# Cross term, table rows, squares and copies rearranged around a serial loop

## Chip, cores and metric

One core of a Trainium2 chip runs the whole program. The metric is the device time of one execution in microseconds (us). The kernel before takes 282.21 us (median of three runs, 282.20 to 282.55).

## What is computed

The input x is (1, 2048, 128). The reference chains four layers; the change touches the first and, by its place in the queues, the second.

```python
def step(M, kv):                     # 2048 tokens, one after the other
    k_t, v_t = kv
    v_pred = jnp.einsum('bf,bfd->bd', k_t, M)
    surprise = jnp.linalg.norm(v_t - v_pred, axis=-1, keepdims=True)
    delta = k_t[:, :, None] * v_t[:, None, :]
    M = M + eta_c[None, :, None] * surprise[:, :, None] * delta
    return (_ln2(M), None)           # subtract the mean, divide by the deviation
...
mem_out = jnp.einsum('btf,bfd->btd', q, M)      # q = phi(x_norm Wq)
output = x + jnp.einsum('btd,ed->bte', mem_out, Wout)
# then: expert layer (expert 1 of 16), h = relu(x W1 + b1), y = h W2 + b2
# then: causal attention with fractional rotary turns, one head
# then: a gated network with ternary weights, 128 -> 512 -> 512 -> 512 -> 128
```

## The kernel before

Tokens are the chunks of 128 of the large tiles x and xn (16 chunks); banks are the eight accumulation banks of TensorE, 512 fp32 each. The recurrence over 2048 tokens is replaced by 128 lanes (one on each partition) that each run over 32 tokens (L = 32), overlapping by 16, from products of keys and values. So the body is a loop of 32 steps in which every lane advances by one token, and what a step needs of the products is held in tables by lane.

Every engine has its own program, written out in order; semaphores join them. `o.did` counts an instruction on its engine's own semaphore and `need` waits for one. Around the change:

- **Before the steps.** TensorE brings the Gram products into lanes (L526) and ScalarE copies them into CC (L955). TensorE then multiplies the queries (L533, banks 4 and 5), turns xn (L540, banks 0 to 3), and computes the last rows (L544 to L549, bank 7). It runs eight warm-up matmuls (L445), which compute nothing that is read, and the eight expert-hidden matmuls (L561). ScalarE takes relu, relu of the negative and exp of the queries over both banks (L959 to L962), the first surprise (L970), the four copies of the turned xn into xT (L973), the last rows (L975 to L978), small rows of the tables (L987 to L991), and three of the eight hidden units (L984). VectorE forms lane rows of 32 elements (L1402 to L1410), four outer products (L1393, lines L1411 to L1415), the tables (L1419 to L1433), the near products (L1438), three far products that stay on VectorE (L1450) and row G (L1453).
- **A step j.** VectorE: near pairs (L1481), the scan over 18 rows of ST (L1504), the row of squares (L1486), alpha (L1518), the wide update of four rows (L1536), one diagonal element (L1491), for j < 13 the far product FP into a ring of three buffers (L1544), and the last pair (L1547). From step 13 on the near pairs follow the scan. ScalarE: square root (L1023), copy (L1025), the next surprise (L1028), which the next step's near pairs (from step 13 on its scan) wait for; then in steps 0 to 4 one hidden unit, and in some steps a piece of `behind`.
- **TensorE in the steps.** For j < 13 it adds FP of step j into bank 4 with an identity matmul (L608); VectorE may not rewrite a buffer of the ring before its matmul is done. Between them stand six pieces of `behind` (L577 to L587), which carry tables by one lane, and parts of the first expert output (L595 to L603). Behind them come L617, the three other expert outputs, and four warm-up matmuls for each of the steps 26 to 30. Step 13 of VectorE reads the sums of bank 4 (L1525, L1527).
- **After the steps.** TensorE's L636 waits for the last surprise; VectorE's L1554 waits for L636, and then a short exchange between the engines leads to the memory output (L623) and the attention.

The tiles: Cr holds four rows of 32 for each step, ST the 18 rows of the scan (R_G, R_T and so on are its row numbers), Y the pair sums, VC, aT, bT, V, KAP, FUS and Dv are tables and rows by lane; O1 to O4 and TA to TC are temporary squares of 16 x 32.

## Time and profile before

| | before |
|---|---|
| median of three runs | 282.21 us |
| the profiled execution | 282.72 us, span 280.9 us |
| TensorE matmuls busy | 264.1 us, 94% |
| VectorE busy | 219.0 us, 78% |
| ScalarE busy | 193.0 us, 69% |
| GpSimd busy | 98.5 us, 35% |
| mean granted clock of TensorE | 0.987 |
| chain that ended last | PE 67%, DVE 23%, ACT 4%, issue 3%, DMA 2% |

In the rows PE is TensorE's matmuls, PEld its weight loads, DVE VectorE, ACT ScalarE, POOL GpSimd. A busy share is a mean over stages that have different limits, so the stages have to be read one by one. In a timeline a row merges like instructions in sequence: their start, the time from the first start to the last end, and their count. An instruction's duration contains a latency that overlaps the next one's, so a cost in a queue is read from start to start. An fp32 matmul has two records. In a table of stretches the numbers after the length are busy time and count of PE, PEld, DVE, ACT and POOL, then TensorE's granted clock as a share of full speed.

### The profile page before, as it was taken

How to read it: one execution, taken by the hardware profiler on the slowest of the kernel's cores; microseconds unless marked ns; L12 is line 12 of the kernel's file. 1: busy time of each engine (PE TensorE's matmuls, PEld its weight loads, DVE VectorE, ACT ScalarE, POOL GpSimd, SP SyncE). 2: the span in 40 equal slices, each digit the busy share in tenths (PEclk: the TensorE clock that was granted, in tenths of full speed). 3: DMA queues.
4: the chain of work that ended last, by engine and by line, in shares of the span. 5: the costliest groups of instructions: out<-in, count | busy, mean ns of one | idle time of the engine just before them, and what ended most of it. 6: DMA issues, size and time to landing. Idle time of an engine off the chain costs nothing.

```text
span 280.9 us, 5415 instructions
## 1 busy us (share of the span) xinstructions
PE 264.1 (94%) x1799; PEld 170.1 (61%) x1803; DVE 219.0 (78%) x742; ACT 193.0 (69%) x469; POOL 98.5 (35%) x122
## 2 busy tenths in 40 slices
PE   6899898899999889979999999999999999999993
PEld 2369863354645544746877777787695444444482
DVE  6977389999998689589999988778852766666684
ACT  1587469865456459778865799999674877777730
POOL 9210000000000055998885469898872000000000
PEclk9999979999999979999999999999999999999999
DMA  8700000000000091300000000000000000000005
GB/s 204 199 13 2 2 2 1 0 1 0 2 1 1 13 387 54 128 23 1 2 2 0 0 2 1 3 0 0 0 2 2 0 0 1 2 1 0 0 10 144
DMA packets 8287, 8.51 MB, mean 30 GB/s; under 512 B 1729, under 2 KB 7362, under 8 KB 7746
## 3 DMA queue, kind: packets, MB, share of 16 engines
q1 hardware_dynamic: 7826, 7.84, 8.7%
q10 hardware_dynamic: 432, 0.30, 0.4%
q8 instruction: 16, 0.26, 0.4%
q14 instruction: 13, 0.11, 0.1%
HBM read 7.09 MB, written 1.05 MB: 29 GB/s over the span
## 4 chain that ended last, share of the span: by engine, by line
PE 67%; DVE 23%; ACT 4%; issue 3%; DMA 2%; SPq 0%; DVEq 0%; ACTq 0%
PE PS L826 10%; PE PS L827 10%; PE PS L784 10%; PE PS L764 9%; PE PS L775 4%; PE PS L480 3%; PE PS L499 3%; DVE arena L1536 2%; DVE arena L1481 2%; PE PS L741 2%; PE PS L742 2%; PE PS L704 2%; PE PS L445 2%; DMA x<-L_attn_x 2%; DVE arena L1518 1%
## 5 line engine op out<-in xcount | busy, mean ns | idle before, releaser
L826 PE MATMUL PS<-arena 128*128 128x512 f16 x128 | 48.5, 379 | 0.6 <-issue 0.6
L827 PE MATMUL PS<-arena 128*128 128x512 f16 x128 | 48.5, 379 | 0.0
L1768 DVE TENSOR_TENSOR arena<-arena 128x512 f32<-128x512 f32 x32 | 22.2, 692 | 19.5 <-ACT arena L1203 19.5
L764 PE MATMUL PS<-arena 128*128 128x512 f32 (+3 forms) x80 | 32.0, 531 | 0.0
L1202 ACT ACTIVATE arena<-PS,arena 128x512 f32<-128x512 f32 x32 | 22.0, 688 | 13.1 <-PE PS L827 13.1
L1251 POOL CAST arena<-arena 128x512 f16<-128x512 f32 x2 | 1.2, 612 | 78.9 <-ACT x L1064 78.9
L1243 POOL TENSOR_TENSOR arena<-arena 128x256 f32<-128x256 f32 x32 | 21.6, 674 | 15.5 <-DVE arena L1707 13.2
L1176 ACT ACTIVATE arena<-PS,lnt 128x512 f32<-128x512 f32 (+3 forms) x40 | 25.0, 635 | 1.8 <-DVE lnt L1722 1.7
L1244 POOL TENSOR_TENSOR arena<-arena,small 128x256 f16<-128x256 f32 (+1 forms) x36 | 23.8, 662 | 2.8
L1715 DVE TENSOR_REDUCE mxb<-PS 128x1 f32<-128x512 f32 (+3 forms) x40 | 22.1, 602 | 1.6 <-PE PS L766 1.6
L826 PEld LDWEIGHTS PS<-arena 128*128 128x128 f16 x128 | 12.5, 98 | 15.7 <-issue 0.7
L1203 ACT ACTIVATE arena<-PS,arena 128x512 f16<-128x512 f32 x32 | 21.8, 682 | 0.0
L827 PEld LDWEIGHTS PS<-arena 128*128 128x128 f16 x128 | 12.5, 98 | 15.0
L764 PEld LDWEIGHTS PS<-arena 128*128 128x128 f32 x80 | 14.0, 190 | 11.7 <-issue 9.5
L775 PE MATMUL PS<-con,arena 128*128 128x128 f32 x136 | 19.6, 274 | 0.5 <-ACT arena L1176 0.5
L784 PE MATMUL PS<-arena,xn 128*128 128x128 f32 x144 | 19.3, 279 | 0.4 <-ACT xn L1160 0.3
L784 PEld LDWEIGHTS PS<-arena,xn 128*128 128x128 f32 x144 | 17.4, 191 | 1.4 <-ACT xn L1160 1.1
L784 PE MATMUL PS<-arena 128*128 128x128 f32 x128 | 17.3, 279 | 0.3 <-ACT arena L1160 0.2
L775 PEld LDWEIGHTS PS<-con,arena 128*128 128x128 f32 x136 | 15.1, 141 | 3.7 <-issue 1.7
L1699 DVE SCALAR_TENSOR_TENSOR arena<-arena,PS 128x256 f32<-128x256 f32 x32 | 13.4, 420 | 4.6 <-ACT arena L1133 3.9
L445 PE MATMUL PS<-warm 128*128 128x512 bf16 x49 | 13.6, 413 | 3.5 <-POOL warm L1223 1.3
L1700 DVE SCALAR_TENSOR_TENSOR arena<-PS,arena 128x256 f32<-128x256 f32 x32 | 15.5, 484 | 1.1
(282 smaller groups left out, 638.0 us busy)
## 6 DMA issues: line engine op xcount, KB each, us to landing
arena<-h_T SPq DMA_DIRECT2D x2, 1024.0 KB, 5.5
x<-L_attn_x SPq DMA_DIRECT2D x4, 256.0 KB, 4.6
arena<-cos SPq DMA_DIRECT2D x1, 1024.0 KB, 4.8
arena<-sin SPq DMA_DIRECT2D x1, 1024.0 KB, 7.0
out<-arena SPq DMA_DIRECT2D x4, 256.0 KB, 2.3
arena<-w_T SPq DMA_DIRECT2D x3, 256.0 KB, 2.9
con<-shape_constants ACTq DMA_DIRECT2D x1, 192.0 KB, 3.4
w1e<-L_ffn_W SPq DMA_DIRECT2D x1, 128.0 KB
```

The source lines that it names most:

```text
L764: i = mm(PS[:, k, 0:cnt * P], qT1[:, t * P:(t + 1) * P], kT1[:, c * P:(c + cnt) * P], start=True, stop=not last)
L775: i = tr(PS[:, 4 + gi % 2, (b - c) * P:(b - c + 1) * P], Pr[t % 2][:, b * P:(b + 1) * P], ident)
L784: i = mm(PS[:, 7, (t % 4) * D:(t % 4 + 1) * D], PT[t % 2][:, b * P:(b + 1) * P], V1[:, b, :], start=(b == 0), stop=(b == t))
L826: mm(bank(u % 8), wH[:, k, m * P:(m + 1) * P], sH[:, k, cols], start=(k == 0), stop=False)
L827: i = mm(bank(u % 8), wL[:, k, m * P:(m + 1) * P], sL[:, k, cols], start=False, stop=(k == HT4 - 1))
L1176: f(Pr[t % 2][:, c * P:(c + cnt) * P], PS[:, SCORE_BANK[gi], 0:cnt * P], ACT.Exp, scale=1.0 / D, bias=nbs[:, t:t + 1], accum_out=rsums[:, ...
L1202: f(FP[u % 4], bank(u % 8), ACT.Gelu, scale=s_[:, u % HT4:u % HT4 + 1])
L1203: f(high, bank(u % 8), ACT.Gelu, scale=s_[:, u % HT4:u % HT4 + 1]).then_inc(read, 1)
L1243: o.need(o.did(tt(rest, value, high, ALU.subtract)))
L1244: return tt(low, rest, low_scale.broadcast_to([P, cols]), ALU.mult)
L1715: i = did(v.tensor_reduce(mxb[:, gi:gi + 1], PS[:, SCORE_BANK[gi], 0:cnt * P], AX.X, ALU.max))
L1768: v.tensor_tensor(RP[m], FP[m], high, ALU.subtract).then_inc(rest_ready, 1)
```

## The change

The cross term of the mean (a V D products, formerly TA, O2 and the row built from them for all pairs) is no longer formed as a table: Cr row 1 is built from aT and VC alone, a new row R_W of ST holds the other factor, a new row R_M receives the product in the last operation of each step, which becomes three columns wide, and the next surprise reads R_M instead of R_D. Row R_CD of ST is made by VectorE from two small operations. Rows 2 and 3 of Cr are sums of two squares each, now added by TensorE with identity matmuls into banks 2 and 3 and copied by ScalarE. The row of squares and the diagonal element become one operation over two rows of the arena, for which ST is moved next to Cr. On ScalarE the query relus are split by bank, the four copies into xT and all eight hidden units go into the steps 0 to 8, and the pieces of `behind` two steps later. On TensorE the second half of the hidden matmuls follows the far products of the steps 0 to 3; the last rows (bank 6 now) follow L617, and ScalarE copies them in the steps 15 to 18.

The diff, cut:

```diff
@@ -352,8 +354,13 @@
         LANE_RUNS = [(0, 5), (5, 5), (10, 5), (15, 2)]
 
 
-        BEHIND_AT = {4: (0,), 5: (1,), 6: (2,), 8: (3,), 9: (4,), 10: (5,)}
+        BEHIND_AT = {6: (0,), 7: (1,), 8: (2,), 10: (3,), 11: (4,), 12: (5,)}
+        EXPERT_AT = {0: (("x", 0), ("x", 1)), 1: (("x", 2), ("h", 0)), 2: (("x", 3), ("h", 1)), 3: (("h", 2),), 4: (("h", 3),), 5: (("h", 4),), 6: (("h", 5),), 7: (("h", 6),), 8: (("h", 7),)}
+        LAST_AT = 15
         BEHIND_BANK = (5, 6, 7, 5, 6, 7)
+
+
+        TERM_BANK = (2, 3)
 
         def values_in(engine, ch):
...
                     i = mm(PS[64 * hf:64 * hf + F, 4 + b, :], wqT[:, :], xrT[:, ch * BANK:(ch + 1) * BANK], start=True, stop=True)
-            i.then_inc(q_done, 1)
+                i.then_inc(q_done, 1)
+
+            def table(k):
+
+                b = TERM_BANK[k]
+                for i in range(2):
+                    if i == 0:
+                        pe.wait_ge(lanes_act, b + 1)
+                    pe.wait_ge(terms_ready, 2 * i + k + 1)
+                    p = mm(bank(b), ident, (O4, O3, TC, TB)[2 * i + k].rearrange("p j t -> p (j t)"), start=(i == 0), stop=(i == 1))
+                p.then_inc(terms_done, 1)
+
+            table(0)
+            table(1)
 
             pe.wait_ge(xn_ready, NT)
             for n in range(NT):
                 if n % 4 == 0:
                     pe.wait_ge(lanes_act, n // 4 + 1)
+                    if n // 4 in TERM_BANK:
+                        pe.wait_ge(terms_act, TERM_BANK.index(n // 4) + 1)
...
-
-            pe.wait_ge(mrow_ready, 1)
-            mm(PS[0:L, 7, F + 2 * D:F + 2 * D + 1], lane[:, MM, :], con[:, C_ID + LAST:C_ID + LAST + 1], start=True, stop=True).then_inc(last_done, 1)
-
             keep_warm(8, 6)
             pe.wait_ge(moe_in, 64)
-            for h in range(2):
-                for ch in range(4):
-                    if h == 0:
-                        pe.wait_ge(xnt_act, ch + 1)
-                    if (h, ch) == (0, 0):
-                        pe.wait_ge(qphi_act, 2)
-                    if (h, ch) == (0, 3):
-                        pe.wait_ge(last_act, 4)
-                    mm(bank((4, 0)[h] + ch), w1e[:, h * P:(h + 1) * P], xT[:, ch * BANK:(ch + 1) * BANK], start=True, stop=True).then_inc(eh_done, 1)
+
+            def expert_hidden(h, ch):
+
+                pe.wait_ge(xnt_act, ch + 1)
+                mm(bank((4, 0)[h] + ch), w1e[:, h * P:(h + 1) * P], xT[:, ch * BANK:(ch + 1) * BANK], start=True, stop=True).then_inc(eh_done, 1)
...
@@ -602,19 +618,28 @@
                         for h in range(2):
                             mm(PS[:, c, (n % 4) * P:(n % 4 + 1) * P], HT[:, h, n * P:(n + 1) * P], w2e[:, h, :], start=False, stop=False)
 
-            pe.wait_ge(eh_act, 4)
             for j in range(FAR):
+                pe.wait_ge(eh_act, min(j + 1, 4))
                 pe.wait_ge(fp_ready, j + 1)
                 mm(PS[:, FAR_BANK, j * HALF:(L - 1) * HALF], ident, FPf[j % N_FP][:, 0:(L - 1 - j) * HALF], start=(j == 0), stop=(j == FAR - 1)).then_inc(far_done, 1)
+                if j < 4:
+                    expert_hidden(1, j)
                 for k in BEHIND_AT.get(j, ()):
                     behind(k)
                 if j in EO_EARLY:
-                    pe.wait_ge(eh_act, 8)
+                    pe.wait_ge(eh_act, 5 if EO_EARLY[j][1] == 1 else 8)
                     expert_output(0, *EO_EARLY[j])
 
             pe.wait_ge(small_in, 16 * 13)
             pe.wait_ge(behind_act, 9)
             mm(PS[:, 7, 0:D], wvT2, wo, start=True, stop=True).then_inc(wvo_done, 1)
+            tr(PS[0:L, 6, 0:F], KU[F:P, SH - 2, 1, :], con[F:P, C_ID + F:C_ID + P])
+            mm(PS[0:L, 6, F:F + D], VT[:, T - L:T], woutT[:, :], start=True, stop=True)
+            mm(PS[0:L, 6, F + D:F + 2 * D], ones[:, 0:L], woutT[:, :], start=True, stop=True).then_inc(last_done, 1)
+
+            pe.wait_ge(mrow_ready, 1)
+            mm(PS[0:L, 6, F + 2 * D:F + 2 * D + 1], lane[:, MM, :], con[:, C_ID + LAST:C_ID + LAST + 1], start=True, stop=True).then_inc(last_done, 1)
+
             def memory_output(two, first, end):
...
 
-            zq = PS[:, 4:6, :].rearrange("p b c -> p (b c)")
+            def relus(b, negative):
+
...
+
+                act.wait_ge(terms_done, k + 1)
+                have = bank(TERM_BANK[k]).rearrange("p (j t) -> p j t", t=L)
+                if k == 0:
+                    f(Cr[:, 0:HALF, 2, 0:L - 1], have[:, :, 1:L], ACT.Copy).then_inc(terms_act, 1)
+                else:
+                    f(Cr[:, 0:HALF, 3, :], have, ACT.Copy).then_inc(terms_act, 1)
+
             act.wait_ge(q_done, 1)
-            f(QT, zq, ACT.Relu).then_inc(qphi_act, 1)
-            n = o.did(f(QE, zq, ACT.Relu, scale=-1.0))
+            n = relus(0, True)
+            relus(0, False)
             o.need(n)
-            f(QE, QE, ACT.Exp, scale=-1.0).then_inc(qphi_act, 1)
+            f(QE[:, 0:BANK], QE[:, 0:BANK], ACT.Exp, scale=-1.0).then_inc(qphi_act, 1)
+            act.wait_ge(q_done, 2)
+            n = relus(1, True)
+            o.need(n)
+            f(QE[:, BANK:2 * BANK], QE[:, BANK:2 * BANK], ACT.Exp, scale=-1.0).then_inc(qphi_act, 1)
+            table(0)
 
             def surprise(j):
...
             act.wait_ge(lanes_act, 1)
             f(surprise(0), CC[:, 2, 1, 0:1].broadcast_to([W, SCAN // STEP]), ACT.Sqrt).then_inc(g_ready, 1)
-            for ch in range(4):
+            table(1)
+            act.wait_ge(terms_act, 1)
+            o.did(f(lane[:, VB, 0:HALF], of_tables(2), ACT.Square))
+            o.did(f(ST[:, R_C, PAD:PAD + HALF], of_tables(2), ACT.Copy, scale=2.0))
+            act.wait_ge(terms_act, 2)
+            o.did(f(ST[:, R_B, PAD:PAD + HALF], of_tables(3), ACT.Copy, scale=0.5))
+            n = o.did(f(lane[:, T0, 0:HALF], of_tables(3), ACT.Relu, scale=0.5))
+            assert n == STATICS
+            relus(1, False)
+
+            def last_rows(i):
+
+                if i == 0:
+                    act.wait_ge(last_done, 2)
+                to, have, scale = ((U_LAST, PS[0:L, 6, 0:F], 1.0), (VW, PS[0:L, 6, F:F + D], 1.0), (WSUM, PS[0:L, 6, F + D:F + 2 * D], 1.0),
+                                   (negm, PS[0:L, 6, F + 2 * D:F + 2 * D + 1], -1.0))[i]
+                f(to, have, ACT.Copy, scale=scale).then_inc(last_act, 1)
+
+            def normed_turned(ch):
+
                 act.wait_ge(xnt_done, ch + 1)
                 f(xT[:, ch * BANK:(ch + 1) * BANK], bank(ch), ACT.Copy).then_inc(xnt_act, 1)
-            act.wait_ge(last_done, 2)
-            f(U_LAST, PS[0:L, 7, 0:F], ACT.Copy).then_inc(last_act, 1)
-            f(VW, PS[0:L, 7, F:F + D], ACT.Copy).then_inc(last_act, 1)
-            f(WSUM, PS[0:L, 7, F + D:F + 2 * D], ACT.Copy).then_inc(last_act, 1)
-            f(negm, PS[0:L, 7, F + 2 * D:F + 2 * D + 1], ACT.Copy, scale=-1.0).then_inc(last_act, 1)
-
...
-            act.wait_ge(tables_ready, 1)
-            o.did(f(lane[:, VB, 0:HALF], of_tables(2), ACT.Square))
-            o.did(f(ST[:, R_C, PAD:PAD + HALF], of_tables(2), ACT.Copy, scale=2.0))
-            o.did(f(ST[:, R_B, PAD:PAD + HALF], of_tables(3), ACT.Copy, scale=0.5))
-            o.did(f(ST[:, R_CD, PAD:PAD + HALF], of_tables(1), ACT.Copy))
-            n = o.did(f(lane[:, T0, 0:HALF], of_tables(3), ACT.Relu, scale=0.5))
-            assert n == STATICS
             act.wait_ge(moe_in, 64)
-            for u in range(8 - EH_LATE):
-                hidden(u // 4, u % 4)
 
             def behind(k):
...
                     act.wait_ge(h_ready, j + 1)
                     f(surprise(j + 1), HS[:, j + 1:j + 2].broadcast_to([W, SCAN // STEP]), ACT.Sqrt,
-                      scale=of_scan(R_D), bias=AL[:, j:j + 1]).then_inc(g_ready, 1)
-                if j < EH_LATE:
-                    hidden((8 - EH_LATE + j) // 4, (8 - EH_LATE + j) % 4)
+                      scale=of_scan(R_M), bias=AL[:, j:j + 1]).then_inc(g_ready, 1)
+                for what, i in EXPERT_AT.get(j, ()):
+                    (normed_turned(i) if what == "x" else hidden(i // 4, i % 4))
+                if 0 <= j - LAST_AT < 4:
+                    last_rows(j - LAST_AT)
                 if j == SB_AT:
...
-            did(v.tensor_tensor(R[FD], FUS, Dv, ALU.mult))
-            did(v.tensor_tensor(R[KD], KAP, Dv, ALU.mult))
             did(v.tensor_scalar(R[WJ], Dv, float(1.0 / np.sqrt(D)), None, ALU.mult))
-            last()
+            need(fd)
+            did(v.tensor_scalar(R[MZ], R[FD], float(-np.sqrt(D)) / N, None, ALU.mult))
+            mr = did(v.tensor_scalar(R[MR], R[FD], -2.0 / N / N, None, ALU.mult))
             v.tensor_scalar(R[MM], R[FD], 1.0 / N, None, ALU.mult).then_inc(mrow_ready, 1)
-            did(v.tensor_scalar(R[MZ], R[FD], float(np.sqrt(D)) / N, None, ALU.mult))
-            did(v.tensor_scalar(R[M2], R[FD], 2.0 / N, None, ALU.mult))
-            did(v.tensor_scalar(R[MR], R[FD], -2.0 / N / N, None, ALU.mult))
-            did(outer(O1, Dv, R[VB]))
-            need(o.n - 1)
-            did(outer(O2, R[M2], R[KD]))
-            did(outer(O3, R[MR], R[FD]))
-            did(outer(O4, R[MZ], KAP))
+            did(v.tensor_scalar(ST[:, R_W, PAD:PAD + L - 1], Dv[:, 1:L], float(-2.0 / np.sqrt(D)), None, ALU.mult))
+            need(mr)
+            outer(O4, R[MZ], KAP).then_inc(terms_ready, 1)
+            outer(O3, R[MR], R[FD]).then_inc(terms_ready, 1)
+            o1 = did(outer(O1, Dv, R[VB]))
             dve.wait_ge(lanes_act, 4)
-            outers = o.n
-            need(outers)
-            ab = did(v.tensor_tensor(TA, aT, V, ALU.mult))
+            v.tensor_tensor(TC, aT, R[WJ][:, 0:HALF].unsqueeze(2).broadcast_to(SQUARE), ALU.mult).then_inc(terms_ready, 1)
+            v.scalar_tensor_tensor(out=TB, in0=bT, scalar=2.0 / N, in1=V, op0=ALU.mult, op1=ALU.mult).then_inc(terms_ready, 1)
+            need(o1)
             vc = did(v.scalar_tensor_tensor(out=VC, in0=V, scalar=2.0, in1=O1, op0=ALU.mult, op1=ALU.subtract))
-            bv = did(v.tensor_tensor(TB, bT, V, ALU.mult))
-            aw = did(v.tensor_tensor(TC, aT, R[WJ][:, 0:HALF].unsqueeze(2).broadcast_to(SQUARE), ALU.mult))
             did(v.tensor_copy(VJ[:, 0:HALF], diagonal(2)))
+            square = did(v.tensor_tensor(R[T1][:, 0:HALF], diagonal(0, 1), diagonal(0, 1), ALU.mult))
             need(vc)
             half = did(v.tensor_scalar(vc_diagonal, vc_diagonal, 0.5, None, ALU.mult))
-            square = did(v.tensor_tensor(R[T1][:, 0:HALF], diagonal(0, 1), diagonal(0, 1), ALU.mult))
-            did(v.scalar_tensor_tensor(out=Cr[:, 0:HALF, 1, 0:L - 1], in0=TA[:, :, 1:L], scalar=-2.0, in1=O2[:, :, 1:L], op0=ALU.mult, op1=ALU.add))
-            need(bv)
-            c1_ = did(v.scalar_tensor_tensor(out=Cr[:, 0:HALF, 3, :], in0=TB, scalar=2.0 / N, in1=O3, op0=ALU.mult, op1=ALU.add))
-            need(aw)
-            v.tensor_tensor(Cr[:, 0:HALF, 2, 0:L - 1], TC[:, :, 1:L], O4[:, :, 1:L], ALU.subtract).then_inc(tables_ready, 1)
-            need(c1_)
+            need(half)
+            v.scalar_tensor_tensor(out=Cr[:, 0:HALF, 1, 0:L - 1], in0=aT[:, :, 1:L], scalar=-1.0, in1=VC[:, :, 1:L], op0=ALU.mult, op1=ALU.mult).then_inc(tables_ready, 1)
             statics = did(v.tensor_tensor(R[T1][:, 0:HALF], R[T1][:, 0:HALF], vc_diagonal, ALU.mult))
 
             for j in range(HALF - 2):
...
 
+            dve.wait_ge(tables_ready, 1)
+            dve.wait_ge(terms_act, 1)
+            cross = did(v.tensor_tensor(R[WT][:, 0:HALF], ST[:, R_W, PAD:PAD + HALF], of_tables(2), ALU.mult))
             for j in range(FAR, HALF):
                 did(v.tensor_tensor(OJF[j - FAR], *far_factors(j), ALU.mult))
+            need(cross)
+            did(v.tensor_tensor(ST[:, R_CD, PAD:PAD + HALF], R[WT][:, 0:HALF], of_tables(1), ALU.add))
             need(statics)
             dve.wait_ge(act_order, STATICS)
...
             def query_sums(*pieces):
 
-                dve.wait_ge(qphi_act, 2)
+                dve.wait_ge(qphi_act, 4)
                 for q in pieces:
...
-                def row_of_squares():
+                def squares():
 
                     need(added)
-                    return did(v.tensor_tensor(Cr[:, j, 0, j + 1:end - 1], CC[:, 0, j + 1, j + 2:end], Y[:, j, j + 2:end], ALU.mult))
-
-                def diagonal_term():
-
-                    need(added)
-                    did(v.tensor_tensor(ST[:, R_T, PAD + j + 1:PAD + j + 2], CC[:, 0, j + 2, j + 2:j + 3], Y[:, j + 1, j + 2:j + 3], ALU.mult))
+                    a0 = cr_at + j * 4 * L + j + 1
+                    apart = st_at + R_T * RW + PAD + j + 1 - a0
+                    both = arena[:, a0:a0 + 2 * apart].rearrange("p (l t) -> p l t", l=2)[:, :, 0:end - j - 2]
+                    return did(v.tensor_tensor(both, CC[:, 0, j + 1:j + 3, j + 2:end], Y[:, j:j + 2, j + 2:end], ALU.mult))
 
                 if j == HALF:
...
-                    diagonal_term()
                 if j < FAR:
 
...
                                            op0=ALU.mult, op1=ALU.mult).then_inc(fp_ready, 1)
                 need(formed)
-                formed = did(v.tensor_tensor(ST[:, R_X:R_SQ + 1:STEP, PAD + j + 1], ST[:, R_R, PAD + j + 1:PAD + j + 2].broadcast_to([W, 2]),
-                                             ST[:, R_C:R_R + 1, PAD + j + 1], ALU.mult))
+                formed = did(v.tensor_tensor(ST[:, R_X:R_M + 1:STEP, PAD + j + 1], ST[:, R_R, PAD + j + 1:PAD + j + 2].broadcast_to([W, 3]),
+                                             ST[:, R_C:R_W + 1, PAD + j + 1], ALU.mult))
                 if Q_AT <= j < Q_AT + 6:
```

## Rows read from the trace of the kernel before

**Rows 1.** Chain of work, 83 to 92 us: start us, us, engine, tile, line

```profile
86.56 4.25 PE PS L445 x19
...
90.81 0.21 PE PS L636 x2
```

**Rows 2.** Stretches: length, busy us (x instructions) by engine, PEclk, DMA share, GB/s

```profile
51.60:67.30 15.70, 14.45 (x45) 7.21 (x43) 15.70 (x88) 11.82 (x46) 0.00 (x0) 1.00 0.00 1
...
67.30:90.80 23.50, 23.40 (x110) 13.26 (x112) 21.98 (x137) 12.55 (x56) 0.00 (x0) 1.00 0.01 1
```

**Rows 3.** Timeline of ScalarE: table load, copies, second step, last root

```profile
42.65 1.28 ACT L970 ACT_TABLE_LOAD   x1
...
44.05 2.04 ACT L973 ACTIVATE xT<-PS 128x512 f32<-128x512 f32 x4
...
50.07 0.20 ACT L1023 ACTIVATE arena<-arena 128x1 f32<-128x1 f32 x1
...
50.66 0.67 ACT L984 ACTIVATE arena<-PS,b1e 128x512 f32<-128x512 f32 x1
...
89.96 0.40 ACT L1028 ACTIVATE arena<-arena 128x6 f32<-128x6 f32 x1
```

**Rows 4.** Timeline of TensorE: start us, us, engine, line, operation, operands, xcount, [idle before]

```profile
44.73 7.10 PE L561 MATMUL PS<-xT,w1e 128*128 128x512 f32 x16 [0.71 <-issue]
...
51.67 2.58 PE L608 MATMUL PS<-arena,con 128*128 128x496 f32 x6
...
67.96 1.02 PE L597 MATMUL PS<-xn,con 128*128 128x512 f32 x2
...
72.08 1.02 PE L595 MATMUL PS<-x,con 128*128 128x512 f32 x2
```

**Rows 5.** Timeline of VectorE before the steps

```profile
35.88 0.18 DVE L1402 TENSOR_SCALAR arena<-arena 128x32 f32<-128x32 f32 x1 [1.55 <-ACT arena L955]
...
36.73 2.49 DVE L1393 TENSOR_TENSOR arena<-arena 128x512 f32<-128x512 f32 x4
...
39.33 0.69 DVE L1419 TENSOR_TENSOR arena<-arena 128x512 f32<-128x512 f32 x1
...
43.87 2.21 DVE L1438 TENSOR_TENSOR arena<-arena 128x210 f32<-128x210 f32 x14
...
46.00 1.14 DVE L1450 TENSOR_TENSOR arena<-arena 128x288 f32<-128x288 f32 x3
...
47.62 0.44 DVE L1481 SCALAR_TENSOR_TENSOR arena<-arena 128x210 f32<-128x210 f32 x1 [0.21 <-DVE arena L1453]
```

**Rows 6.** Timeline of VectorE in the second step

```profile
49.52 0.41 DVE L1481 SCALAR_TENSOR_TENSOR arena<-arena 128x182 f32<-128x182 f32 x1
...
50.46 0.15 DVE L1491 TENSOR_TENSOR arena<-arena 128x1 f32<-128x1 f32 x1
...
50.53 0.71 DVE L1544 SCALAR_TENSOR_TENSOR arena<-arena 128x480 f32<-128x480 f32 x1
...
51.23 0.38 DVE L1481 SCALAR_TENSOR_TENSOR arena<-arena 128x156 f32<-128x156 f32 x1
```

**Rows 7.** Timeline of VectorE in a late step

```profile
83.75 0.25 DVE L1536 SCALAR_TENSOR_TENSOR arena<-arena 128x28 f32<-128x28 f32 x1
...
83.91 0.15 DVE L1491 TENSOR_TENSOR arena<-arena 128x1 f32<-128x1 f32 x1
...
84.03 0.16 DVE L1547 TENSOR_TENSOR arena<-arena 128x2 f32<-128x2 f32 x1
```

**Rows 8.** Timeline of TensorE, the block L544 to L549

```profile
41.37 0.23 PE L544 MATMUL PS<-con,arena 64*32 64x64 f32 x1
...
41.99 0.20 PE L549 MATMUL PS<-con,arena 128*32 128x1 f32 x2
```

**Rows 9.** Stretches around the fall of TensorE's granted clock

```profile
33.70:34.50 0.80, 0.08 (x2) 0.06 (x2) 0.62 (x2) 0.39 (x2) 0.00 (x0) 1.00 0.00 0
...
34.80:38.00 3.20, 3.20 (x19) 2.36 (x19) 2.09 (x11) 1.94 (x4) 0.00 (x0) 0.50 0.00 0
```

33 lines of the change are left out of this document (20 added, 13 removed).

## The prediction

> **What bounds the kernel now.** I read the chain of work in order of time first. From 35.9 to 86.56 us nearly every link is a VectorE instruction, and then, before the last step ends, the chain crosses to TensorE: 4.25 us of warm-up matmuls (L445), and only then L636, which releases the next VectorE instruction [rows 1]. So two engines have to be followed. The table of stretches says the same: VectorE is busy throughout 51.6 to 67.3, while TensorE has 1.3 us of idle there; from 67.3 to 90.8 TensorE is busy for 23.40 of 23.50 us [rows 2]. TensorE's queue is full from the last far product on, through the expert outputs and twenty warm-up matmuls (20 x 512 columns back to back, 4.27 us), and ends at 90.81, 0.4 us after ScalarE wrote the last step's root (89.96 + 0.40 [rows 3]), for which L636 waits as well. Both ends are nearly tied; a change that frees VectorE alone gains nothing behind 67.3 unless TensorE's queue too is shorter or starts earlier.
>
> TensorE's order is fixed: eight expert-hidden matmuls (L561) from 44.73 to 51.67, 0.85 us each; thirteen far products (L608) with the six pieces of `behind` and one expert matmul between them, to 67.96; then expert outputs from 67.96 on, the last three from 72.08 [rows 4].
>
> **VectorE before the steps.** Before: eight lane operations of 0.1 from 35.88, four outer products from 36.73 at 0.60 pitch, seven 512-wide ones, `near`, OJF, and the first step at 47.62 [rows 5]. The change has seven lane operations (fd, VB, WJ, MZ, MR, MM, R_W), three outers, and TC, TB, VC, Cr1: seven 512-wide operations in place of eleven. That is 4 x 0.60 = 2.4 less, 0.1 less of lane work and about 0.1 less of waiting for the outers; against it stand the new wait of Cr1 for `half` (0.1), and two 16-wide operations, cross and CD (0.2). New walk: O4 36.52, O3 37.12, O1 37.72, TC 38.32, TB 38.92, VC 39.52, small ones 40.13, Cr1 40.55, near 41.23, OJF 43.45, CD 44.5, G 44.6, and the first step at 45.0. It begins 2.6 us earlier.
>
> It needs ScalarE and TensorE to follow. The two table rows are now four identity matmuls of 0.85 in the queue behind the query matmuls: 39.47 to 42.9. ScalarE's work on the queries ended at 42.65 [rows 3]; now the first bank is released by itself, about 1.0 earlier, and the last relu (0.5) moves behind the rows, so it is free at about 41.2. It copies row 2 at 41.4 (TensorE's end of it) to 42.0, then pays the load of the square root's tables (1.28, as before [rows 3]) to 43.3, copies row 3 to 44.0, and ends the four small rows at 44.4, 0.2 before VectorE asks. So the cover is thin: were the tables 0.5 late, the first step would be 0.3 late. TensorE turns xn at 42.9 to 44.8 and warms up to 46.5.
>
> **The steps 0 to 12.** One step is 49.52 to 51.23 = 1.71 us, and the diagonal takes 0.07 of it (50.46 to the far product at 50.53) [rows 6]. Without it 1.65. The pair of squares reads up to 14 more elements, 0.01, beside the wait for alpha; the third column of the last operation I take at nothing (it has 2 elements now). For VectorE alone: 13 x 0.06 = 0.8.
>
> But now the four copies of xT are in ScalarE's part of the steps. In a step ScalarE starts at the scan's end (50.07) and is free for a copy 0.59 later (50.66) [rows 3]. The copy of x takes 0.5 (2.04 for four), a hidden one 0.57. Scan 0 ends at 45.55: x0 46.17 to 46.75, x1 to 47.25. Scan 1: x2 47.83 to 48.40, h0 to 48.97. Scan 2 ended at 48.82, so ScalarE comes at 48.9: x3 49.50 to 50.10.
>
> **TensorE behind that.** First hidden matmul at 46.85 where it was 44.73, that is 2.1 later. Three of them run to 49.41, then TensorE waits 0.7 for x3. From 50.17 its queue has no gap, by my walk: hidden(0,3) and the four of the second half, 5 x 0.853 = 4.27; the far products, 496 to 304 columns in steps of 16, 5200 columns at 1.67 ns (2.41 us for the first 1440, L608's row of six less its tail of 0.17) = 8.7; `behind` 2240 columns by the same rate, plus 0.4 for the floors of its three narrow ones = 4.2; the expert's first matmul 0.85. In sum 13.7, ending at 68.1. The other bound of that work is what the table shows for it: 14.45 busy [rows 2] and 0.61 for the last far product = 15.1, in which short pauses each leave a tail and a restart. I take 13.7, since the new queue has no such pauses.
> The ring of three far buffers now holds VectorE: L1544 of step 3 waits for the matmul of step 0, which ends at 51.9, where it would be ready at 51.0. ScalarE also waits in step 10 for the third piece of `behind`. Both delays cost nothing, because the far sums in step 13 wait for TensorE's 68.0 anyway (VectorE would be there at 66 to 67). Read at 68.2, where they were read at 68.46, they leave 0.3 of the vector gain of 3.4.
>
> **The steps 13 to 30.** There the diagonal costs nothing now: the last operation starts at 84.03, just when the wide one ends (83.75 + 0.25), and the diagonal at 83.91 lies inside [rows 7]. Taking it out gives 0. The squares, on the path here, grow by 16 elements falling to 1, 136 in all: at about 1 ns, +0.14. The vector chain ends 0.2 earlier than now.
>
> A rule of the Trainium skill ("Perfetto Trace Analysis", Optimizing Scalar/DVE Operations) says that grouping small vector operations raises throughput where the engine is saturated. By it all thirty merged diagonals would count, 2 us at 0.07. The trace agrees for the first thirteen [rows 6] and shows nothing to gain in the rest [rows 7].
>
> **The block that moves.** L544 to L549, 0.82 us (41.37 to 42.19) [rows 8], ran where TensorE had slack and now stands behind L617, in the full stretch. ScalarE's four small copies of it go into steps 15 to 18; it may wait for the block until 73.3 in step 15, 0.1 behind its normal start and within the slack before alpha. They cost nothing. The matmuls cost their whole 0.82.
>
> **The sum.** TensorE: 50.17 + 4.27 + 13.7 + 22.85 (67.96 to 90.81, unchanged work) + 0.82 = 91.8, where L636 now starts at 90.81. So +1.0 us. All that follows hangs on L636 and shifts as a whole. The profiled execution took 282.72 (span 280.9), so it would be 283.7; against the median of 282.21 that gives **283.2**. With a vector walk off by 0.3 either way, the matmuls 0.2 cheaper or 1.4 dearer: 282.8 to 284.6.
>
> **Rivals.**
> *Vector gains carry* (7%). If TensorE made up its late start, the end would follow VectorE: 2.6 + 0.8 + 0.2 for step 0, where ScalarE was late, less 0.1: 3.5 faster, 278.7. It decides at the far sums: TensorE must end L608 by 65, that is 50.2 to 65 for 18 us of matmuls. For it speaks that VectorE is the busier engine up to 67.3; against it the columns. A half form, in which x3 comes before 49 and pauses in the second half that I took for work vanish, gives 280 to 281.6. The same skill section has it that work may well go from a saturated VectorE to another engine; that is this rival, and it holds only if that other engine has room.
> *The tie absorbs it* (14%), 282.0 to 282.7. The late start is 0.5 less than I say and the 0.82 block falls partly into a gap in the new queue (TensorE waiting for VectorE near step 12).
> *ScalarE is late* (11%). It is a link in everything: two relus, table copies, table load and small rows, with 0.2 of cover; then two copies a step. If x3 comes 0.8 to 1.5 later: 284.0 to 284.8.
> *TensorE's clock* (8%). After its pause from 33.7 to 34.5 the granted clock is 0.50, the lower of its two levels (1.2 GHz), from 34.8 to 38.0 [rows 9]. The change puts pauses of 0.35 and 0.7 before a stretch that TensorE bounds. One such fall costs half of 3.3 us: +1.6, 284.8 to 285. Against it: the pause of 0.7 before 44.73 has no fall behind it. The Trainium skill ("TensorE: Matmul & The Clock Gate", Part 1) states that idleness throttles the array and activity releases it; the trace agrees [rows 9], and the rule speaks against moving the copies that feed the matmuls.
> *The tables are no faster summed by TensorE* is within the third.
>
> **How the numbers follow.** Forecast 60% (282.8 to 283.9 within it). The range from 282.2 to 284.7 leaves out the faster rival, the clock and a part of the third: under 2 in 10. A measurement can tell about 0.2%, 0.56 us: faster 0.07, same 0.15, slower 0.78.
>
> **What would show it.** The first step near 45.0 (L1481 before); L561's first at 46.9 and a pause of about 0.7 before its fourth; from 50.2 to L636 a TensorE without idle; L1544 of the fourth step with idle before it, released by TensorE; far sums read near 68.2; the moved block near 72.4, and L636 near 91.8. Wrong it would be if TensorE has idle between 52 and 68, if the first hidden matmul starts before 46, or if the warm-up matmuls in front of L636 start on a scan and not on the end of the expert outputs.

## Result and profile after

The changed kernel takes 283.89 us (median of 5 runs, 283.68 to 284.29), the kernel before 282.21 (5 runs, 282.03 to 282.55). The ratio is 1.0058, with a 95% interval of 1.0044 to 1.0073: it is slower, by 1.7 us. The profiled execution of after took 283.77, span 282.0.

The profile's page of after gives its busy times and its chain by engine:

```profile
PE 265.2 (94%) x1807; PEld 170.0 (60%) x1811; DVE 215.8 (77%) x709; ACT 193.2 (69%) x473; POOL 98.4 (35%) x122
...
PE 77%; DVE 13%; ACT 5%; issue 2%; DMA 2%; SPq 0%; DVEq 0%; ACTq 0%
```

The stretches of after (columns as in [rows 2]): first the pause and the stretch behind it that answer to [rows 9], then from the fourth hidden matmul to the reading of the far sums, and from there to the matmul that was L636 and is now L661:

```profile
33.70:34.50 0.80, 0.09 (x2) 0.02 (x1) 0.66 (x2) 0.39 (x2) 0.00 (x0) 1.00 0.00 0
34.80:38.00 3.20, 3.20 (x25) 1.71 (x23) 2.25 (x10) 2.56 (x6) 0.00 (x0) 1.00 0.00 0
...
50.20:68.30 18.10, 18.10 (x55) 9.91 (x56) 15.19 (x75) 13.50 (x49) 0.00 (x0) 1.00 0.00 0
68.30:92.20 23.90, 23.85 (x117) 13.66 (x116) 20.55 (x113) 12.94 (x59) 0.00 (x0) 1.00 0.00 1
```

TensorE is busy for 18.10 of 18.10 us and then for 23.85 of 23.90. VectorE, which was busy for all of 51.6 to 67.3 before [rows 2], is now busy for 15.19 of 18.10. The bound has gone wholly to TensorE.

The timeline of TensorE in after (columns as in [rows 4]):

```profile
37.90 3.86 PE L550 MATMUL PS<-arena,con 128*128 128x512 f32 x8
41.60 1.91 PE L562 MATMUL PS<-con,xn 128*128 128x128 f32 x16
43.56 1.67 PE L452 MATMUL PS<-warm 128*128 128x512 bf16 x7
47.10 2.81 PE L572 MATMUL PS<-xT,w1e 128*128 128x512 f32 x6 [1.86 <-ACT xT L1037]
50.19 1.13 PE L572 MATMUL PS<-xT,w1e 128*128 128x512 f32 x2 [0.27 <-ACT xT L1037]
51.15 1.00 PE L624 MATMUL PS<-arena,con 128*128 128x496 f32 x2
...
68.47 1.05 PE L613 MATMUL PS<-xn,con 128*128 128x512 f32 x2
...
72.71 0.23 PE L636 MATMUL PS<-con,arena 64*32 64x64 f32 x1
...
73.46 1.13 PE L611 MATMUL PS<-x,con 128*128 128x512 f32 x2
...
88.03 4.26 PE L452 MATMUL PS<-warm 128*128 128x512 bf16 x19
92.22 0.28 PE L661 MATMUL PS<-con,arena 128*32 128x1 f32 x2
```

The expert-hidden matmuls start at 47.10 where they started at 44.73 [rows 4], and TensorE stands 1.86 us for ScalarE's first copy of xT. The matmul that all else hangs on (L636 before, L661 after) is called the decisive one below. The chain of work has it at 90.81 in before [rows 1], but a timeline counts its start a little earlier. As all starts below are from timelines, the row to compare with is this one of before:

```profile
90.74 0.28 PE L636 MATMUL PS<-con,arena 128*32 128x1 f32 x2
```

So the decisive matmul starts at 92.22 instead of 90.74, 1.48 later. From there to the end of the span the kernels take nearly the same: 190.16 us before, 189.78 after.

VectorE in after: the outer products, the last wide table operation, the first step, the far product of the fourth step, the far sums, and the closing operation of a late step. They answer to [rows 5] and [rows 7]:

```profile
36.37 1.89 DVE L1444 TENSOR_TENSOR arena<-arena 128x512 f32<-128x512 f32 x3
...
41.07 2.21 DVE L1481 TENSOR_TENSOR arena<-arena 128x210 f32<-128x210 f32 x14
...
44.83 0.44 DVE L1529 SCALAR_TENSOR_TENSOR arena<-arena 128x210 f32<-128x210 f32 x1 [0.22 <-DVE arena L1501]
...
52.18 0.68 DVE L1587 SCALAR_TENSOR_TENSOR arena<-arena 128x448 f32<-128x448 f32 x1 [1.42 <-PE PS L624]
...
65.80 0.23 DVE L1529 SCALAR_TENSOR_TENSOR arena<-arena 128x6 f32<-128x6 f32 x1 [1.07 <-ACT arena L1077]
...
68.48 0.51 DVE L1571 SCALAR_TENSOR_TENSOR arena<-arena,PS 128x288 f32<-128x288 f32 x1 [0.19 <-PE PS L624]
...
83.26 0.17 DVE L1590 TENSOR_TENSOR arena<-arena 128x3 f32<-128x3 f32 x1
```

ScalarE in after, answering to [rows 3]: table load, the first step with two copies of xT behind its root, the last copy, the last step's root:

```profile
40.68 1.28 ACT L1015 ACT_TABLE_LOAD   x1
...
45.79 0.20 ACT L1072 ACTIVATE arena<-arena 128x1 f32<-128x1 f32 x1 [2.15 <-DVE arena L1550]
...
46.38 1.06 ACT L1037 ACTIVATE xT<-PS 128x512 f32<-128x512 f32 x2
...
49.56 0.57 ACT L1037 ACTIVATE xT<-PS 128x512 f32<-128x512 f32 x1
...
90.31 0.40 ACT L1077 ACTIVATE arena<-arena 128x6 f32<-128x6 f32 x1
```

VectorE enters the steps 2.8 us earlier (44.83 for 47.62) and loses all of it, and what the merging saves in the steps too: 1.42 at L1587 for a far buffer, some 0.1 before the same operation in each of the next five steps, 1.07 in the thirteenth step for ScalarE, and 0.19 before the far sums, which are read at 68.48. VectorE has to wait for TensorE there.

**One caution on the clock.** The granted clock of TensorE differs between executions of one and the same program. The profiled execution of before has two stretches of 3.4 us at half clock (called falls below), [rows 9] and one from 99.7 to 103; that of after has none. Over the 97 runs of the kernel before that stand beside the experiments, those with a mean clock of 0.998 or more took 281.4 to 282.4 us, those with 0.983 to 0.985 283.7 to 284.2. So below I read the start of the decisive matmul beside the median.

Runs of like clock can also be compared alone. At 0.998 or more, the 24 such runs of the kernel before have a median of 281.87, and the three of after took 283.68 to 283.89. That is 1.9 us, more than the 1.7 of the medians.

### The profile page after: what moved, and what is told of

Its sections match the earlier page's. It is cut to its first block, busy times and chain, and to the rows that moved or that the text cites. A ratio compares the mean times of both kernels' runs of the same rounds, so it can differ in the third digit from the quotient of the medians.

```text
span 282.0 us, 5418 instructions
## 1 busy us (share of the span) xinstructions
PE 265.2 (94%) x1807; PEld 170.0 (60%) x1811; DVE 215.8 (77%) x709; ACT 193.2 (69%) x473; POOL 98.4 (35%) x122
## 4 chain that ended last, share of the span: by engine, by line
PE 77%; DVE 13%; ACT 5%; issue 2%; DMA 2%; SPq 0%; DVEq 0%; ACTq 0%
PE PS L851 10%; PE PS L852 10%; PE PS L809 10%; PE PS L789 9%; PE PS L800 4%; PE PS L624 3%; PE PS L487 3%; PE PS L619 3%; PE PS L506 3%; PE PS L766 2%; PE PS L767 2%; PE PS L452 2%; PE PS L572 2%; DMA x<-L_attn_x 2%; PE PS L615 1%
## 5 line engine op out<-in xcount | busy, mean ns | idle before, releaser
L452 PE MATMUL PS<-warm 128*128 128x512 bf16 x49 | 14.2, 426 | 3.8 <-POOL warm L1274 1.3
```

## Experiments

The theory, called T in the expectations, is the forecast's: TensorE's queue decides, its late start costs some 2 us, the moved block its own 0.8, and what VectorE gains goes nowhere. The kernel before, run beside each of the three groups of experiments, had medians of 282.26, 282.33 and 282.32 us; after stands at 283.89.

**The block moved back** in front of the hidden matmuls, with its four copies in front of the steps:

```diff
+            tr(PS[0:L, 7, 0:F], KU[F:P, SH - 2, 1, :], con[F:P, C_ID + F:C_ID + P])
...
             keep_warm(8, 6)
...
             mm(PS[:, 7, 0:D], wvT2, wo, start=True, stop=True).then_inc(wvo_done, 1)
-            tr(PS[0:L, 6, 0:F], KU[F:P, SH - 2, 1, :], con[F:P, C_ID + F:C_ID + P])
...
             act.wait_ge(moe_in, 64)
+            for i in range(4):
+                last_rows(i)
```

> Against the changed kernel (283.89 us median). The last rows' four matmuls go back in front of the warm-ups before the steps (bank 7), and ScalarE copies them in its pause before step 0. Theory T (TensorE's queue sets the end from its fourth hidden matmul to L661): the block took 0.75 us of that queue (72.71 to 73.46), so L661 starts 0.75 earlier, at 91.5, and the time is 283.1. Rival V (VectorE's chain or ScalarE's late copies set the end, and the block lies in a gap): 0.0, 283.9.

Measured: 282.77 us (12 runs, 282.33 to 283.47), ratio to before 1.0014 [0.9999, 1.0030]. The timeline of TensorE:

```profile
46.70 2.81 PE L579 MATMUL PS<-xT,w1e 128*128 128x512 f32 x6 [0.63 <-ACT xT L1039]
...
91.07 0.28 PE L663 MATMUL PS<-con,arena 128*32 128x1 f32 x2
```

The decisive matmul is 1.15 earlier than in after (92.22), and the median 1.1 lower. The pause in front of the hidden matmuls has shrunk from 1.86 to 0.63: the block ran inside it. Of the 1.15, 0.19 came in by the fourth hidden matmul, which starts at 50.00 for 50.19, since ScalarE, busy with small rows just before, answered the first scan at once (in after it did not). The rest, 0.96, is the block. Its own matmuls took 0.75 in after (72.71 to 73.46), and some 0.2 more lay in the distances from L635 to the block (0.32, where L635 and the next matmul are 0.22 apart here) and from L611 to L613 behind it (0.96 for 0.86).

**The four copies of xT in front of the steps again**, one of the eight hidden units in each of the first eight steps:

```diff
-        EXPERT_AT = {0: (("x", 0), ("x", 1)), 1: (("x", 2), ("h", 0)), 2: (("x", 3), ("h", 1)), 3: (("h", 2),), 4: (("h", 3),), 5: (("h", 4),), 6: (("h", 5),), 7: (("h", 6),), 8: (("h", 7),)}
+        EXPERT_AT = {0: (("h", 0),), 1: (("h", 1),), 2: (("h", 2),), 3: (("h", 3),), 4: (("h", 4),), 5: (("h", 5),), 6: (("h", 6),), 7: (("h", 7),)}
...
             act.wait_ge(moe_in, 64)
+            for ch in range(4):
+                normed_turned(ch)
```

> Against the changed kernel (283.89). The four copies of the turned xn go back before step 0, into ScalarE's pause from 43.6 to 45.8; the hidden units follow one a step from step 0. Theory T: the first hidden matmul starts when the warm-ups end, 45.25 where it was 47.10, and the pause before the fourth disappears, so the fourth starts at 47.8 where it was 50.19; all behind it in TensorE's queue is 2.4 earlier, and the time is 281.5. If only the later start counts and the pause comes back elsewhere: 1.85 earlier, 282.0. Rival V (VectorE's steps set the end): its steps 0 to 12 begin no earlier, 283.6 to 283.9.

Measured: 281.20 us (12 runs, 280.9 to 284.7), ratio 0.9976 [0.9950, 1.0003]. TensorE, then VectorE behind the decisive matmul:

```profile
45.10 3.60 PE L572 MATMUL PS<-xT,w1e 128*128 128x512 f32 x8
...
89.61 0.28 PE L661 MATMUL PS<-con,arena 128*32 128x1 f32 x2
```

```profile
65.87 0.52 DVE L1573 SCALAR_TENSOR_TENSOR arena<-arena,PS 128x288 f32<-128x288 f32 x1 [0.19 <-PE PS L624]
...
89.93 0.15 DVE L1599 COPY arena<-PS 32x1 f32<-32x1 f32 x1 [1.54 <-PE PS L661]
```

The hidden matmuls start 2.00 earlier than in after, and the pause before the fourth is gone; the decisive one starts 2.61 earlier, and the median falls by 2.69. No warm-up and no operation of VectorE was taken out. So the copies' place alone is worth more than the whole loss of the change. The interval of the ratio still reaches just over 1; the runs at a clock of 0.998 or more took 281.12 to 281.23, against the 281.87 of before and the 283.77 of after (medians at that clock). VectorE still waits 1.54 for TensorE at the end: more gain of VectorE would give nothing here either.

**Both undone together.**

> Both edits, the block in front of the warm-ups and the copies before step 0. Theory T: 0.75 and 2.4 add up only if the block doesn't push the hidden matmuls; it does so by 0.75 (the warm-ups end at 46.0), so that the fourth starts at 48.6, 1.6 earlier than in the changed kernel, and the block's 0.75 is saved later: 2.35 in sum, 281.5, equal to the copies alone. Were the warm-ups no cover and the block free: 280.8. Rival V: 283.6 to 283.9.

Measured: 281.29 us (12 runs, 281.08 to 281.49), ratio 0.9964 [0.9948, 0.9981]. TensorE:

```profile
45.95 3.60 PE L579 MATMUL PS<-xT,w1e 128*128 128x512 f32 x8
...
89.52 0.28 PE L663 MATMUL PS<-con,arena 128*32 128x1 f32 x2
```

The two edits don't add: 1.1 and 2.7 apart, 2.6 together. With the copies back the queue is full from 43.4 on, in front as behind; the block in front moves the hidden matmuls from 45.10 to 45.95 and saves as much later. Its place costs only where the old place had idle time. What is left of the change beats the kernel before by 1.0 us in the medians, and by 0.7 in runs at 0.998 or more (281.14 for 281.87).

**The diagonal in an operation of its own again**, the rest as in after:

```diff
-                    return did(v.tensor_tensor(both, CC[:, 0, j + 1:j + 3, j + 2:end], Y[:, j:j + 2, j + 2:end], ALU.mult))
+                    return did(v.tensor_tensor(Cr[:, j, 0, j + 1:end - 1], CC[:, 0, j + 1, j + 2:end], Y[:, j, j + 2:end], ALU.mult))
...
+                if n > 0 and j != FAR:
+                    diagonal_term()
```

> Against the changed kernel (283.89). The row of squares and the diagonal element are two operations again; all else as changed. It adds 30 VectorE operations, 0.07 us each in the first thirteen steps. Theory T: VectorE waits 1.4 us for the ring's first buffer and 0.2 for the far sums, so 0.9 more in steps 0 to 12 delays copies x2 and x3 by 0.07 and 0.14 and nothing else: 283.9 to 284.1. Rival V: 0.9 slower, 284.8.

Measured: 284.00 us (10 runs, 283.74 to 285.95), ratio 1.0066 [1.0044, 1.0088]. TensorE at the end, VectorE's far sums, and ScalarE's last root:

```profile
92.08 0.28 PE L661 MATMUL PS<-con,arena 128*32 128x1 f32 x2
```

```profile
68.34 0.51 DVE L1573 SCALAR_TENSOR_TENSOR arena<-arena,PS 128x288 f32<-128x288 f32 x1
```

```profile
89.88 0.39 ACT L1077 ACTIVATE arena<-arena 128x6 f32<-128x6 f32 x1
```

Thirty more operations of VectorE cost 0.1 us, within the error. The rival, in which the merging saves time on the path of this kernel, predicts 284.8 and is refuted. Behind the far sums the apart form is even the shorter: 21.54 us from their start to the last root's, against 21.83 in after (90.31 - 68.48).

**The same merging, put into the kernel before** (its table of squares placed so that one operation reaches both; nothing else of the change):

```diff
+        st_at = at[0]
+        STf = take(SCAN * RW)
         VC = take(HALF * L).rearrange("p (j t) -> p j t", j=HALF)
...
-                if n > 0 and j != FAR:
-                    diagonal_term()
```

> The kernel before with one part of the change alone: the row of squares and the diagonal element are one operation (with ST moved next to Cr). Theory T: in the kernel before TensorE has 1.3 us of pauses in the steps 3 to 12, so here the steps' 0.07 count until its queue is full: the last far product can start 0.6 earlier (when the one before it ends, 66.75, where it was 67.35), the queue behind it moves as a whole, L636 starts at 90.2: 0.6 faster, 281.6. Rival V (all thirty merged operations count): 0.9 to 2.1 faster, 280.1 to 281.3. Rival N (no part of the merge reaches the end): 282.2.

Measured: 281.22 us (12 runs, 280.77 to 283.36), ratio 0.9961 [0.9936, 0.9985]. TensorE:

```profile
43.27 7.10 PE L563 MATMUL PS<-xT,w1e 128*128 128x512 f32 x16 [0.70 <-issue]
...
89.62 0.28 PE L638 MATMUL PS<-con,arena 128*32 128x1 f32 x2
```

Here VectorE leads up to the far sums, so the merging does pay: 1.1 us in the median. How much of it is the merging? The second row needs care. The profiled execution of before started L636 at 90.74, but it held the fall of [rows 9]; an execution without that fall, in the last experiment below, started it at 90.21. So of the 1.12 between 90.74 and 89.62, 0.6 is the merging and 0.5 the absent fall. The runs at a clock of 0.998 or more agree: a median of 281.16 (five runs) for 281.87, 0.7 less. So the merging is worth 0.6 to 0.7, not 1.1.

And 281.22 is also what the whole change gives with its two late parts undone (281.29), so the shorter work of VectorE before the steps brings nothing more at the end. TensorE's row shows what stands against it: the hidden matmuls start at 43.27 here and at 45.95 there, behind the four matmuls that sum the table rows (L550, 37.90 to 41.60 in after). No run leaves those sums with VectorE, so what their move to TensorE costs is not measured by itself.

**The copies moved into the steps, in the kernel before**, and with them, as in after, all hidden units, the second half of the hidden matmuls and the pieces of `behind`; tables, squares and the block stay as before:

```diff
-            for ch in range(4):
-                act.wait_ge(xnt_done, ch + 1)
-                f(xT[:, ch * BANK:(ch + 1) * BANK], bank(ch), ACT.Copy).then_inc(xnt_act, 1)
...
+                for what, i in EXPERT_AT.get(j, ()):
+                    (normed_turned(i) if what == "x" else hidden(i // 4, i % 4))
```

> The kernel before with another part alone: ScalarE's copies of the turned xn and all hidden units in the steps, the second half of the hidden matmuls behind the far products, the pieces of behind two steps later; tables, squares and the last rows as before. Theory T: the first copy waits for the scan of step 0, which ends 2.7 later here than in the changed kernel, and the fourth hidden matmul starts near 52.9 (50.19 in the changed kernel, 46.0 and more in the kernel before, where all eight were through at 51.67). From there TensorE's work is that of the changed kernel less the block (0.75): L636 near 94.2 where it was 90.81, 3.4 slower, 285.6. Rival V: ScalarE has room in the steps and VectorE hardly waits, 282.2 to 282.8.

Measured: 287.88 us (6 runs, 287.51 to 288.84), ratio 1.0186 [1.0151, 1.0221]. TensorE, and a stretch around the end of its pause:

```profile
49.57 5.75 PE L558 MATMUL PS<-xT,w1e 128*128 128x512 f32 x8 [7.12 <-ACT xT L985]
55.16 0.99 PE L611 MATMUL PS<-arena,con 128*128 128x496 f32 x2
...
95.29 0.28 PE L641 MATMUL PS<-con,arena 128*32 128x1 f32 x2
```

```profile
47.50:53.00 5.50, 3.43 (x4) 1.51 (x5) 5.02 (x24) 4.05 (x14) 0.00 (x0) 0.50 0.00 1
```

TensorE stands 7.12 us where it stood 1.86 in after, for two reasons: the first copy comes 2.5 later, since the steps begin later, and TensorE is there 2.8 earlier, since it has no table rows to sum (3.7 us in after) and only the block, 0.8, in their place. The granted clock fell to 0.50, 1.2 GHz, inside this pause, at 46.9, and came back at 53.7. The first four hidden matmuls took 5.59 from start to start (49.57 to 55.16), where they took 3.44 with the copies first (45.10 to 48.54). So the decisive matmul came 1.1 later than the 94.2 expected. The median missed the 285.6 expected by 2.3; the rest lies behind, where the profile has a second fall from 104.9 on, and all six runs had a clock of 0.982 or less. In the change the copies' place costs less than here, because VectorE's shorter work before the steps brings the steps forward.

**One warm-up matmul fewer in each of the last five steps**, in after:

```diff
                 elif EO_AT[-1] + 4 < j < L - 1:
-                    keep_warm(4, 4)
+                    keep_warm(3, 4)
```

> Against the changed kernel (283.89 us median). Three warm-up matmuls instead of four for each of the steps 26 to 30, five fewer in all at the queue's end. Theory T (TensorE's queue sets the end): L661 starts 5 x 0.213 = 1.07 earlier, 91.15, still behind the last root (90.71), so 282.8. Rival V (the vector chain sets it, and the warm-ups fill time in which TensorE would wait): 283.9. Rival C: with fewer of them TensorE's granted clock falls behind the steps, 284 to 285.

Measured: 283.95 us (12 runs, 282.59 to 285.59), ratio 1.0052 [1.0024, 1.0079]. TensorE:

```profile
87.75 3.40 PE L452 MATMUL PS<-warm 128*128 128x512 bf16 x15
91.08 0.28 PE L661 MATMUL PS<-con,arena 128*32 128x1 f32 x2
```

The decisive matmul is earlier by 1.14, near the 1.07 expected, and still the median stays. The runs show why: the two with a mean clock of 0.998 took 282.59 and 282.80, the expected time; seven with 0.982 to 0.989 took 283.04 to 285.59. In the profile the clock is at half for most of 101.7 to 105.3 (from 101.5 to 104.9):

```profile
101.70:105.30 3.60, 3.60 (x9) 1.60 (x8) 2.77 (x14) 1.68 (x5) 3.43 (x4) 0.56 1.00 414
```

**All that pays, together:** both parts undone, 4 warm-up matmuls in place of 8 in front of the hidden ones, 3 in place of 4 in the last steps:

```diff
-            keep_warm(8, 6)
+            keep_warm(4, 6)
...
-                    keep_warm(4, 4)
+                    keep_warm(3, 4)
```

> The changed kernel with copies and block in front of the steps (as in the run with both), and only four warm-ups there (the block takes the place of the other four) and three for each of the steps 26 to 30. Leaving warm-ups out changes nothing that is computed. Theory T: hidden matmuls start at 45.1, 0.85 earlier than with both edits alone, and the tail is 1.07 shorter, so TensorE could be at L663 at 87.6 (89.52 with both); then the last root, near 88.1, is what L663 waits for: 1.4 less than 281.29, that is 279.9. If TensorE's queue were not the bound: 281.3. If the granted clock falls for lack of warm-ups: 281 and more.

Measured: 281.29 us (12 runs, 279.75 to 283.59), ratio 0.9962 [0.9932, 0.9991]. TensorE:

```profile
87.39 0.82 PE L452 MATMUL PS<-warm 128*128 128x512 bf16 x3 [0.20 <-DVE arena L1556]
88.40 0.28 PE L663 MATMUL PS<-con,arena 128*32 128x1 f32 x2 [0.20 <-DVE arena L1556]
```

Now TensorE waits for VectorE's scan before the last warm-ups: the bound has crossed back, and this start, 88.40, is 3.8 earlier than in after. At a clock of 0.997 or more it takes 279.75, 279.98 and 280.58, near the 279.9 expected; nine of the twelve runs had a lower one, and the median is no better than with both undone.

**Is it the missing warm-ups at the end that bring the falls?** The same with 4 warm-ups in the last steps:

> As the run with both edits and four warm-ups in front of the steps, but with all twenty at the end (four for each of the steps 26 to 30). Theory T: TensorE's queue is 1.07 longer than with fifteen, L663 at 88.7 where it waited for the last root until 88.40, so 0.3 slower than that kernel in executions without a fall of the granted clock (279.8 to 280.0 there): 280.2. Theory C (fewer warm-ups at the end make falls of the clock behind them more frequent): the median is nearer to 280.2 and the spread smaller than with fifteen. If the falls have nothing to do with their number: a median near 281 and the same spread.

Measured: 282.56 us (12 runs, 281.11 to 283.79), ratio 0.9999 [0.9975, 1.0024]; the decisive matmul at 88.69. Nine of the twelve runs had a clock of 0.988 or less, where three warm-ups gave five such, and the profile has a fall twice as long as most, from 97.3 to 104.1:

```profile
96.00:103.40 7.40, 5.72 (x14) 3.18 (x16) 5.64 (x33) 3.29 (x9) 3.84 (x4) 0.58 0.93 375
```

So the explanation that fewer warm-ups bring the falls does not hold. At the same clock of 0.994 the two kernels differ little (281.11 to 281.22 here, 281.15 there), as their decisive starts do (0.29); the 1.3 between their medians goes with the clock.

**Seven warm-up matmuls into the short pauses of TensorE behind the loop**, four near 95 and three near 98 us, in three kernels: in the one with three warm-ups for each of the last steps, in after, and in before.

```diff
-            keep_warm(4, 4)
+            keep_warm(8, 4)
             general_path(pe, general)
...
             normed(0)
+            keep_warm(3, 5)
```

> The kernel with both edits, four warm-ups in front and fifteen at the end, and seven more where TensorE pauses behind the memory output: four before the branch (a pause of 2.26 us) and three behind the first turned chunk (a pause of 0.69). They compute nothing. Theory C (the falls of the granted clock at 98 to 102 come from those pauses): all or nearly all executions run as its best ones do, median 279.9. If the falls come from elsewhere: median 281.3 as without them. If the seven lie on the path: up to 1.5 slower than the best ones, 281.4, with little spread.

> The changed kernel with the same seven warm-ups behind the memory output. Theory C: its executions without a fall took 283.7 to 283.9, so the median is 283.8 and those with falls (284.1 to 284.3) are fewer. With the kernel before changed likewise it gives the ratio of the two without falls behind the exchange: theory T says 1.5 us (L661 at 92.22 against 90.74), that is 1.0053.

> The kernel before with the same seven warm-ups behind the memory output. Theory C: its best executions took 281.4 to 281.7 and the median 282.3; falls behind the exchange are kept away, a fall near 35 us is not, and the median comes to 282.0 or less. If the falls come from elsewhere: 282.3 with the same spread.

Measured: 280.79 us (12 runs, 280.14 to 283.28), ratio 0.9953 [0.9922, 0.9983], for the first, the lowest median of all; 283.36 (283.27 to 284.2), 1.0043 [1.0021, 1.0064], in after; 282.62 (281.85 to 284.01), 1.0005 [0.9976, 1.0033], in before. The first still has a fall, now in front of the new warm-ups:

```profile
91.50:95.00 3.50, 3.17 (x33) 3.00 (x31) 1.78 (x11) 1.21 (x3) 0.00 (x0) 0.52 0.02 7
```

In before seven of the twelve runs still had a clock of 0.985 to 0.994, and the times still spread over 2.2 us. In the first two the medians fell by 0.5; in before the median rose by 0.3. That the warm-ups keep the clock up is therefore not shown.

The third gives the baseline that the prediction lacked, a kernel before with no fall in front of its loop. Its TensorE:

```profile
43.10 7.10 PE L561 MATMUL PS<-xT,w1e 128*128 128x512 f32 x16 [0.70 <-issue]
...
90.21 0.28 PE L636 MATMUL PS<-con,arena 128*32 128x1 f32 x2
```

Up to L636 this kernel is the kernel before. Its first step of VectorE starts at 47.26, so that after, with 44.83, is 2.4 earlier than it. At a mean clock of 1.0 it took 281.86 and 282.24, and after with the same warm-ups 283.35 to 283.47: 1.1 to 1.6 us for the change. Without the extra warm-ups it was 1.9 at like clocks, as said above, and the two decisive starts, 92.22 and 90.21, differ by 2.0. The change costs 1.1 to 2.0 us with clocks alike, by what stands behind the loop.

## Why the prediction was right

It forecast 283.2 us, slower with 0.78; measured were 283.89, inside its range, and slower. Its sum put the profiled execution at 283.7; it was 283.77. By its steps:

- **VectorE before the steps.** The first step at 45.0 was forecast, 44.83 measured. The row for the outers is three long and starts 0.36 before its old place; every step of the walk came 0.1 to 0.2 earlier than forecast.
- **Tables by TensorE.** The turning of xn behind them was forecast at 42.9 and started at 41.60, since the fall of [rows 9], which the walk had taken over from the trace of before, did not come. It gave nothing: TensorE waited for ScalarE's first copy anyway, 1.86 us where the forecast had 0.35.
- **ScalarE.** It was ready in time, but took the first scan late: the scan ends at 45.38, L1072 starts at 45.79. 0.03 to 0.04 was assumed. That gave 47.10 for the first hidden matmul, where 46.85 was forecast.
- **The pause before the fourth** took up that error: it was 0.27 where 0.7 was forecast, and the fourth started at 50.19, 50.17 forecast.
- **TensorE without idle from there.** Held: 18.10 busy of 18.10.
- **Hidden matmuls, far products and `behind`.** From the fourth hidden matmul to L613 the forecast had 4.27 + 13.7 = 18.0; measured were 68.47 - 50.19 = 18.3. No single price was far off: the five hidden matmuls took 4.40 for 4.27, the far products 8.8 for 8.7, `behind` 4.2 as forecast and the expert's one 0.86 for 0.85, and the forecast's own terms add to 13.75.
- **Ring of far buffers.** L1587 of the fourth step waited from 50.8 to 52.2, released by TensorE; 51.0 to 51.9 was forecast. ScalarE's wait for `behind` came too: 1.3 us for L599, and with it the 1.07 of VectorE at L1529.
- **The merged diagonal.** That it brings nothing with TensorE as bound was confirmed: apart it costs 0.1 us. The squares' growth was forecast at 0.14 behind the far sums; the apart form is 0.29 shorter there. The last root came at 90.71, 0.35 later than before where 0.2 earlier was forecast. It cost nothing, TensorE being later still.
- **The moved block.** It started at 72.71, 72.4 forecast, and cost 0.96 in its place, 0.82 forecast; moving it back gave 1.1 in the median, of which some 0.2 came by another way, ScalarE's quick answer.
- **L661** started at 92.22, 91.8 forecast: 0.3 from the matmuls up to L613, 0.1 behind them.

**Where it was right by luck.** The forecast's 1.0 us between the two starts was 1.48 measured, and against an execution of before's code without the fall 92.22 - 90.21 = 2.0. Two things are in the gap: 0.5 of small errors (0.4 of mis-sized work, and 0.07 because the sum took the end of before's queue, 90.81, from the chain and its other starts from the timeline), and 0.5 that the fall of [rows 9] had cost the profiled execution of before and that I took for its normal course. The profiled execution of before had a second fall near 100, which the one of after lacks too; that is probably why the spans differ by 1.1 only, and why the 283.7 forecast for the profiled execution came so near to 283.77. That agreement is luck. Against the medians, 1.7 was measured for the 1.0 forecast. The mechanism held; the weak step is the choice of one profiled execution as a baseline without asking what its falls were worth.

**The rivals.** *Vector gains carry* is refuted: all of them were handed back, most of it at two waits, 1.42 for TensorE and 1.07 for ScalarE. The rule of the Trainium skill ("Perfetto Trace Analysis", Optimizing Scalar/DVE Operations), that grouping helps a saturated engine, fits both sides of the measurement: in the kernel before, with VectorE busy throughout up to the far sums, the grouping gave 0.6 in the decisive start and 0.7 in runs of like clock, not the 2 us of all thirty; in after, with VectorE waiting, apart costs 0.1. The *tie* did not absorb the late start, whose undoing gives 2.7. *ScalarE late* happened by 0.4 and ended in the pause before the fourth. *TensorE's clock* did not come true in after: granted 1.00 behind the pauses of 1.86 and 0.27. It did in the kernel before with the copies moved, inside a pause of 7.12. The Trainium skill ("TensorE: Matmul & The Clock Gate", Part 1) says that idleness throttles the array; this pair of traces agrees as to the direction, while the same pause at 33.7 to 34.5 was followed by 0.50 in before [rows 9] and by 1.00 in after.
